# Two attention layers with feed-forward blocks on one core: V's bias folded into the output projections, and ScalarE instead of VectorE taking v out of PSUM

## The reference, cut to what matters

```python
x = x + (y_self + y_cross) @ Wp + bp      # y_self causal, over layernorm(x); y_cross over ctx
x = x + bitlinear_ffn(layernorm(x))       # per-token 8-bit, weights in -1, 0, 1, gelu
x = x + y_cross2 @ Wo + bo                # layer 1, cross-attention over the same ctx
x = x + quantised_ffn(layernorm(x))       # per-tensor 8-bit, gelu
# each attention:
v = heads(src @ Wv + bv)
y = softmax(q k^T * scale) @ v
```

## Time and profile before

| | |
|---|---|
| median of 3 runs | 1823.12 us (1822.88 to 1827.1) |
| profiled execution | 1819.35 us, span 1817.5 us |
| busy share of PE, PEld, DVE, ACT, POOL | 89%, 39%, 76%, 63%, 36% |
| mean granted clock of TensorE | 0.952 |

### The profile page before, as it was taken

One profiled execution on the slowest core, in us unless ns is written; L12 is line 12 of the kernel. 1 busy time (PEld: TensorE's weight loads), 2 busy tenths in 40 slices (PEclk: granted clock), 3 DMA queues, 4 the chain that ended last, 5 costly groups with the idle time before them and its releaser, 6 DMA issues.

```text
span 1817.5 us, 28822 instructions
## 1 busy us (share of the span) xinstructions
PE 1618.0 (89%) x9552; PEld 706.3 (39%) x9552; DVE 1389.3 (76%) x3221; ACT 1147.5 (63%) x2178; POOL 659.3 (36%) x918
## 2 busy tenths in 40 slices
PE   5898889998999989998999999988999997899677
PEld 1334334423443434433443344433443443333236
DVE  6678868788687787778787778878588787687287
ACT  1475485567765685667665685657655855765497
POOL 3436223551454134631454134623562242310140
PEclk7899889999999999999999999999999998999898
DMA  7444313323232323332242323332332232133113
GB/s 190 129 115 126 79 36 100 88 74 97 57 110 75 94 60 100 88 111 60 71 117 65 82 77 91 88 103 74 85 106 60 54 99 50 45 85 132 48 69 117
DMA packets 106949, 159.46 MB, mean 88 GB/s; under 512 B 20657, under 2 KB 83249, under 8 KB 106801
## 3 DMA queue, kind: packets, MB, share of 16 engines
q1 hardware_dynamic: 101904, 156.43, 30.9%
q10 hardware_dynamic: 4896, 1.18, 0.3%
HBM read 105.00 MB, written 51.38 MB: 86 GB/s over the span
## 4 chain that ended last, share of the span: by engine, by line
PE 56%; DVE 18%; ACT 12%; POOL 6%; issue 5%; DMA 2%; ACTq 1%; SPq 0%; DVEq 0%; POOLq 0%
PE acc L1511 12%; PE st L1497 11%; PE misc L1478 10%; PE misc L1454 7%; DVE nmax L1277 6%; PE misc L1426 4%; ACT probs L1003 4%; PE misc L1538 3%; PE misc L1466 3%; ACT tail_h L1073 2%; DVE misc L1271 2%; ACT hq L1032 2%; ACT tail_h L1058 1%; PE misc L1565 1%; PE misc L1552 1%
## 5 line engine op out<-in xcount | busy, mean ns | idle before, releaser
L1003 ACT ACTIVATE probs<-st 128x512 f32<-128x512 f32 (+3 forms) x1536 | 758.1, 552 | 373.7 <-PE st L1497 233.6
L1277 DVE TENSOR_REDUCE nmax<-misc 128x1 f32<-128x512 f32 x1024 | 651.0, 683 | 165.4 <-PE misc L1478 162.6
L1478 PE MATMUL misc<-stack 96*128 96x512 bf16 (+3 forms) x1536 | 525.9, 365 | 71.5 <-DVE nmax L1277 45.4
L1497 PE MATMUL st<-stack 99*128 99x512 bf16 (+3 forms) x1536 | 543.4, 364 | 42.2 <-ACT probs L1003 36.3
L1271 DVE CUSTOM_DVE_ANT_0 misc<-misc,mask_mx 128x384 f32<-128x384 f32 (+3 forms) x512 | 239.9, 517 | 99.4 <-PE misc L1478 95.0
L1497 PEld LDWEIGHTS st<-stack 99*128 99x128 bf16 x1536 | 149.3, 99 | 384.8 <-ACT probs L1003 231.6
L1478 PEld LDWEIGHTS misc<-stack 96*128 96x128 bf16 x1536 | 148.2, 100 | 222.2 <-DVE nmax L1277 85.6
L882 POOL TENSOR_TENSOR parts<-qk,zero 128x512 bf16<-128x512 f32 x78 | 81.5, 1044 | 216.3 <-ACT qk L986 216.3
L1511 PE MATMUL acc<-probs,v_x 128*32 128x512 f32 x1152 | 158.6, 623 | 0.0
L1511 PE MATMUL acc<-probs,v_s 128*32 128x512 f32 (+3 forms) x1152 | 117.1, 479 | 0.1
L1500 PE MATMUL st<-mask_st,identb 128*128 128x128 bf16 x512 | 112.7, 223 | 0.0
(11 more groups left out here) (264 smaller groups left out, 2098.9 us busy)
## 6 DMA issues: line engine op xcount, KB each, us to landing
parts_xk<-parts SPq DMA_DIRECT2D x54, 128.0 KB
parts_xq<-parts SPq DMA_DIRECT2D x54, 128.0 KB
stack<-parts_xq SPq DMA_DIRECT2D x36, 192.0 KB, 3.2
stack<-parts_xk SPq DMA_DIRECT2D x36, 192.0 KB, 3.6
parts_sk<-parts SPq DMA_DIRECT2D x48, 128.0 KB
parts_sq<-parts SPq DMA_DIRECT2D x48, 128.0 KB
stack<-parts_sq SPq DMA_DIRECT2D x32, 192.0 KB, 2.8
stack<-parts_sk SPq DMA_DIRECT2D x32, 192.0 KB, 3.5
```

Of the source, the lines that this page charges most:

```text
L1003: act.activation(probs[:, j % P_SLOTS, c, T - w:], st_bank(n, 4 * j + c)[:, 0:w], ACT.Exp, scale=SCALE).then_inc(exp_done, 1)
L1277: dve.tensor_reduce(nmax[:, ring, first:first + NT * (len(cs) - 1) + 1:NT], src, AX.X, ALU.max, negate=True).then_inc(misc_free[slot], 1)
L1478: last = pe.matmul(o, stack[0:ROWS, r, 0, c, P * i:P * i + P], stack[0:ROWS, r, 1, c, 0:w], start=True, stop=True)
L1497: last = pe.matmul(o[:, 0:w], stack[0:AUG, r, 1, c, P * j:P * j + P], stack[0:AUG, r, 0, c, T - w:T], start=True, stop=not causal)
```

## The change

`v` moves from DVE to ACT: two copies of a whole 128x512 bank for a step in place of four additions of 128x256, and no bias. The three bias vectors are loaded as columns (256 numbers each) instead of rows broadcast over 128 partitions. A new step `fold`, twice, multiplies them by the output projection's weights on PE and adds the result to the row that the residual step adds anyway (`row_Ao`, `row_Co`) on DVE. `values` waits for the two reads of `misc` instead of for `v_done`; the POOL steps that add the two rows wait for `folded` the first time.

```diff
+FOLDS = ["Ao", "Co"]
-        return [("w_load", 1), ("load0", 1)] + slots(us[:1], project(0, "s"), 1, True) + \
+        return [("w_load", 1), ("load0", 1)] + slots(us[:1], project(0, "s") + [("fold", 0, w) for w in FOLDS], 1, True) + \
-    "misc": {"maxima": 1, "weights": 1, "w_row": 1, "w_tot": 1, "ctx_T": 1, "norm_T": 2, "project": 1, "v": 2, "negmax_T": 1, "heads_out": 1,
+    "misc": {"fold": 1, "maxima": 1, "weights": 1, "w_row": 1, "w_tot": 1, "ctx_T": 1, "norm_T": 2, "project": 1, "v": 2, "negmax_T": 1, "heads_out": 1,
-                   "fk": L1_xattn_bk}
+                   "fk": L1_xattn_bk, "sv": L0_xattn_bv, "xv": L0_xattn_bcv, "fv": L1_xattn_bv}
-        rows = {"sv": L0_xattn_bv, "xv": L0_xattn_bcv, "fv": L1_xattn_bv, "Ao": L0_xattn_bp, "Co": L1_xattn_bo,
+        rows = {"Ao": L0_xattn_bp, "Co": L1_xattn_bo,
-        NFIRST = 6
+        NFIRST = 5
-                        if (n == "xv") == first:
+                        if not first:
@@ GpSimd @@
+                if (s.key[1], k) == (0, "C"):
+                    pool.wait_ge(folded, 2)
...
+                if s.key[1] == 0:
+                    pool.wait_ge(folded, 1)
@@ ScalarE @@
+            def v(s):
+                p = s.args[0]
+                for k in range(2):
+                    copy_misc(s, k, v_of(s, p)[:, 2 * k:2 * k + 2, :, 0:D],
+                              lambda b: b[:, :].rearrange("p (t h d) -> p t h d", t=2, h=H))
@@ VectorE @@
-            def v(s):
-                p = s.args[0]
-                bias = Bv[p + "v"][:, :].rearrange("p (h d) -> p h d", d=D)
-                for k in range(2):
-                    wait_misc_full(dve, s, k)
-                    slot = misc_slot(s, k)
-                    for t in range(2):
-                        dve.tensor_tensor(v_of(s, p)[:, 2 * k + t, :, 0:D],
-                                          misc[slot][:, C * t:C * t + C].rearrange("p (h d) -> p h d", d=D), bias,
-                                          ALU.add).then_inc(*((v_done[p], 1) if t == 0 else (misc_free[slot], 1)))
+            def fold(s):
+                row, slot = Bv[s.args[0]], misc_slot(s)
+                wait_misc_full(dve, s)
+                dve.tensor_tensor(row[:, :], misc[slot][:, 0:C], row[:, :], ALU.add).then_inc(folded, 1)
+                dve.wait_ge(folded, FOLDS.index(s.args[0]) + 1)
+                dve.sem_inc(misc_free[slot], 1)
@@ TensorE @@
+            def fold(s):
+                w = s.args[0]
+                kinds = {"Ao": ("sv", "xv"), "Co": ("fv",)}[w]
+                wait_misc_free(pe, s)
+                for kind in kinds:
+                    for k in range(KC):
+                        last = pe.matmul(misc[misc_slot(s)][:, 0:C], Bq[kind][:, k:k + 1].to_broadcast([P, P]), W[w][:, k, :],
+                                         start=(kind, k) == (kinds[0], 0), stop=(kind, k) == (kinds[-1], KC - 1))
+                last.then_inc(misc_full, 1)
...
                 if j == 0:
-                    pe.wait_ge(v_done[p], s.b.times(2, 2).at())
+                    for k in range(2):
+                        wait_misc_read(pe, s, k, ("v", s.unit[0], p))
```

More of the change, by code:

```diff
@@ L522, in two_layers_kernel @@
         biased = sems("biased", "AFC")
-        v_done = sems("v_done", "xsf")
+        folded = sem("folded")
         y_summed = sem("y_summed")
@@ L1044, in down_T @@
                 copy_misc(s, 0, hqT[:, t % 2, :, :].rearrange("p k t -> p (k t)"), as_bf16)
-            walk(act, dict(consts=consts, consts_rest=consts_rest, weights=weights, ctx_T=ctx_T, norm_T=norm_T, project=project, negmax_T=negmax_T, scores=scores,
+            walk(act, dict(consts=consts, consts_rest=consts_rest, weights=weights, ctx_T=ctx_T, norm_T=norm_T, v=v, project=project, negmax_T=negmax_T, scores=scores,
                            heads_copy=heads_copy, y_T=y_T, quant_T=quant_T, gelu=gelu, hid_peak=hid_peak, down_q=down_q,
@@ L1314, in _ @@
             walk(dve, dict(consts=consts, consts_rest=consts_rest, project=project, split=split, w_peak=w_peak, w_row=w_row, w_tot=w_tot, w_ints=w_ints, stats=stats_, norm=norm, x_scale=x_scale, quant_x=quant_x, hidden=hidden,
-                           hid_peak=hid_peak, hid_scale=hid_scale, down=down, v=v, maxima=maxima, heads_out=heads_out,
+                           hid_peak=hid_peak, hid_scale=hid_scale, down=down, fold=fold, maxima=maxima, heads_out=heads_out,
                            residual=residual, finish=finish))
@@ L1566, in down @@
                 last.then_inc(misc_full, 1)
-            walk(pe, dict(consts=consts, consts_rest=consts_rest, weights=weights, w_row=w_row, w_tot=w_tot, ctx_T=ctx_T, norm_T=norm_T, project=project, v=v, maxima=maxima, negmax_T=negmax_T,
+            walk(pe, dict(consts=consts, consts_rest=consts_rest, weights=weights, w_row=w_row, w_tot=w_tot, ctx_T=ctx_T, norm_T=norm_T, project=project, fold=fold, v=v, maxima=maxima, negmax_T=negmax_T,
                           scores=scores, values=values, heads_out=heads_out, y_T=y_T, residual=residual, quant_T=quant_T,
```

## The result

The changed kernel takes 1830.4 us (median of 7 runs, 1829.32 to 1834.16), the kernel before 1823.24 beside it (1821.14 to 1828.18). The ratio is 1.0039, 95% interval 1.0027 to 1.0051, so +7.1 us, between 4.9 and 9.3. The forecast was 1.0033 and 1829.1 us. The sum was right, but three of its larger terms were not, and they partly cancelled.

The account below looks back on a forecast made before the run. PE was taken as the bound, DVE counting only where PE waits. Terms -0.7 + 0 + 1.9 + 2.1 + 1.4 + 0 + 1.3 = +6.0 us, ratio 1.0033, gave 1829.1 us on the median; range 1820 to 1834.

Parts of the forecast that it names:

- The eight gelu places and not the load decide: PE waited for v only beside gelu steps, 5.2 us in all; what ACT holds up counts, not DVE's saved time.
- Steady gelu places, -0.7: At 428, 630, 831 and 1032 us ACT is free; its copy replaces DVE's 0.76 us pair, saving 0.17 each.
- The place at 1240 us, 0: Gelu place where the table load now stands behind two copies; the delay mostly covered, 0, at most 0.5 us.
- The places at 234 and 1408 us, 1.9: Gelu places where ACT works without a break; two copies delay everything behind by 0.97 us, twice.
- The last gelu place, 2.1: At 1540 us v's banks stay unread until the gelus end, so maxima wait and scores come 2.1 us later.
- the third rival: Longer stalls also cost clock: 1.7 us at each of three lengthened gelu places, +11.0 in all, 1834.1 us; chance 0.16.
- "x" steps, +1.4: Copies push an exponential that PE's `values` weight load waits for: 0.2 us at each of seven steps, two of them "f".
- The folds, +1.3: Six f32 matmuls on PE at about 78 us, 0.23 us each, 1.4 together, less overlap: +1.3 us.
- twice that: Upper bound for the fold matmuls on PE, if weight loads and matmuls don't overlap in this form.
- Absorbed by ScalarE's idle time: Rival: ACT, idle 37% of the span, absorbs its copies; +0.6 us remains, 1823.7 us on the median; chance 0.27.
- VectorE is the bound: Rival: DVE's removed v additions save 6.6 us, net -5.8, giving 1817.3 us on the median; chance 0.16.

Follow-up runs that it names:

- e3: The changed kernel with v at three gelu places (234, 1408 and the last) copied by VectorE instead of ScalarE: 1825.65 us, ratio to before 1.0014.
- e1: The changed kernel with its folds kept, but VectorE takes every v with plain copies and ScalarE none: 1826.45 us, ratio to before 1.0025.
- e6: The changed kernel, but at the last gelu place ScalarE copies v between the first and second gelu: 1829.65 us, ratio to before 1.0030.
- e7: The changed kernel with both folds moved early, right behind the constants, and every v copied by VectorE: 1822.71 us, ratio to before 0.9999.
- e8: The changed kernel with folds early, ScalarE copying v only at five gelu places (sequences 2 to 6), VectorE the rest: 1819.86 us, ratio to before 0.9985.

## Why the prediction was right, point by point

- *The eight gelu places and not the load decide*: right. Three places (6 copies) carry 4.6 us by the timed difference of e3, good to 3, and 6.5 by the trace; the steady turns have not become longer. The folds are the other cost, 2.7.
- *Steady gelu places, -0.7*: right (0.16 to 0.17 at each of the four). ScalarE reads a bank of f32 in 0.59 us, VectorE in 0.69 with a plain copy (e1) and in 0.76 with two additions.
- *The place at 1240 us, 0*: right. The first exponential was 0.45 us late, and the next 0.43 less so.
- *The places at 234 and 1408 us, 1.9*: right (0.96 each), with 0.68 more behind the first, at a granted clock of 0.57.
- *The last gelu place, 2.1*: the mechanism was right, the size too small; 3.85. The wait itself came out, 3.51 us for the bank. Behind it the granted clock was 0.57, so maxima, scores and `values` took longer. This looks like the third rival, 1.7 us for each lengthened place; it happened at two of three places with 0.7 and some 1.8 us, and that the stall is its cause is likely and not shown (e6).
- *"x" steps, +1.4*: wrong, about 0. The step that failed is that PE's weight load "waits exactly for that exponential". The row's releaser is inferred, and it named the exponential that came last ahead of the load, not the one that the load needed.
- *The folds, +1.3*: the step that failed is the price, 0.23 us for each of six matmuls: that was the time of a record, and a matmul leaves two. It is twelve records, 2.69 us, the "twice that" which stood as the upper bound but for another reason.
- *Absorbed by ScalarE's idle time*: true for the 16 steps away from a gelu and at five of the eight gelu places, false at three. *VectorE is the bound*: not borne out; the kernel with all of VectorE's old load is no slower than before (e7), and the fastest one has nearly all of it (e8).

Against the forecast the last gelu place has 1.8 us more, the one at 234 us 0.7 more, the "x" steps 1.4 less and the folds 1.4 more. The terms as traced add up to 6.0 + 1.8 + 0.7 - 1.4 + 1.4 = 8.5 us, inside the measured 4.9 to 9.3. That the forecast came within 1.3 us of the median is in part luck: the "x" term was too large by as much as the folds were too small.

On the two readers of PSUM the Trainium skill has a second statement, which the prediction had not drawn on: "VectorE: DVE Perf Modes", in its section on the TRN2 errata, lists for a PSUM source 120 cycles at 0.96 GHz on VectorE and 172 at 1.2 GHz on ScalarE, and on both a cycle for each element where no faster mode applies. For 512 columns, with no faster mode, that is an estimate of 0.66 and 0.57 us. The traces have 0.692 and 0.592: the order agrees, both are some 4 to 5% longer.

## What to carry to other kernels

Work that moves to an engine with a third of its time free costs nothing at most places and everything at the few where that engine has a long uninterrupted run, so look these up one by one, and ask what the late reader holds: here two banks of a ring cost three times as much as the engine's own microsecond. Put one-off work into a wait of the engine that does it. When a price is taken from a trace, count records with records: one f32 matmul of the program leaves two here. Before explaining microseconds between two single traces, take a second trace of the same kernel.

## What the runs showed of the hardware

Where 12 matmul records of other work filled TensorE's wait for the first stack, v behind it took 3.62 us in all five traces, against 4.88 to 6.27 in the seven traces where TensorE stood idle there; the granted clock over that stretch was 0.75 to 0.86 against 0.55 to 0.66. The other way round, TensorE's wait of 3.51 us at the last gelu place was followed by 0.57 in all three traces that have it, against 0.93 behind a wait of 0.68. These are the two levels of 2.4 and 1.2 GHz in different shares. Spells at the lower level also come without a change in the program: the same stretch of the same kernel was at 0.98 in one execution and at 0.92 in another, 3.3 us apart.
